# Second cross attention of a two-layer decoder: the key mask is added in PSUM by VectorE in the pass that takes the row maxima, instead of by a bf16 matmul on TensorE

## What is computed

```python
scale = sqrt(128)
q = (text_hidden @ Wq)      # 16 heads of 128
k = (vision_tokens @ Wk)    # 8 key heads of 128, each shared by 2 heads
v = (vision_tokens @ Wv)
scores = einsum('bhtd,bhsd->bhts', q, k) / scale
scores = where(vision_mask[:, None, None, :], scores, -inf)
attn = nan_to_num(softmax(scores, axis=-1), nan=0.0)
out = einsum('bhts,bhsd->bhtd', attn, v)
x = x + out.reshape(B, T, 16 * 128) @ Wo
```

## Time and profile before

| | |
|---|---|
| time, median of 3 runs | 1762.47 us (1761.71 to 1762.89) |
| time of the profiled execution | 1759.19 us |
| its span in the trace | 1757.4 us |
| PE busy, share of the span | 1602.4 us, 91% |
| DVE | 1055.4 us, 60% |
| ACT | 840.0 us, 48% |
| POOL | 740.1 us, 42% |
| mean granted clock of PE | 0.965 of full speed |
| the 64 steps of this sublayer | 1170.4 to some 1522.6 us, about a fifth of the span |

### The profile page before, as it was taken

The page is one execution under the profiler, slowest core; times in us unless marked ns, Lnnn a source line. Parts: engine busy times, 40 slices in busy tenths (PEclk is TensorE's granted clock), DMA queues, the critical chain, the costliest instruction groups (busy, mean ns, idle before and its releaser), DMA issues. The chain is left out here.

```text
span 1757.4 us, 32678 instructions
## 1 busy us (share of the span) xinstructions
PE 1602.4 (91%) x10512; PEld 1276.1 (73%) x10512; DVE 1055.4 (60%) x2390; ACT 840.0 (48%) x2322; POOL 740.1 (42%) x908
## 2 busy tenths in 40 slices
PE   4999979999999998999968888879999999888887
PEld 2565658888888886888845555469999999767675
DVE  3566645656656564555445666545555555589996
ACT  1434437777776775322224444445555555432221
POOL 3666625555455553232321222103333333357775
PEclk9999989999999999899978999989999999999999
DMA  5000020000000000000030000020000000000000
GB/s 219 1 0 0 1 84 3 4 3 1 3 1 3 1 4 1 20 1 1 1 120 1 0 0 0 1 87 7 7 7 7 6 4 1 1 3 12 9 12 13
DMA packets 15399, 28.71 MB, mean 16 GB/s; under 512 B 1489, under 2 KB 11986, under 8 KB 14546
## 3 DMA queue, kind: packets, MB, share of 16 engines
q1 hardware_dynamic: 15314, 27.63, 4.4%
HBM read 25.53 MB, written 2.10 MB: 16 GB/s over the span
## 5 line engine op out<-in xcount | busy, mean ns | idle before, releaser
L1264 POOL TENSOR_TENSOR weights_even<-weights_even,cross_reciprocal 128x512 f32<-128x512 f32 x64 | 67.1, 1049 | 256.4 <-DVE cross_reciprocal L1382 256.4
L1309 ACT ACTIVATE weights_even<-bank,cross_shift 128x128 f32<-128x128 f32 x256 | 90.7, 367 | 102.1 <-DVE cross_shift L1374 102.1
L843 POOL TENSOR_TENSOR weights_odd_early<-weights_odd_early,cross_reciprocal 128x512 f32<-128x512 f32 x64 | 66.7, 1042 | 167.6 <-DVE cross_reciprocal L969 167.6
L1032 PEld LDWEIGHTS bank<-ident,weights_odd_early 128*128 128x128 f32 x768 | 93.7, 141 | 44.4 <-issue 32.7
L1100 PE MATMUL bank<-weights_odd_early 128*128 128x256 f32 x512 | 121.7, 380 | 2.1 <-ACT weights_odd_early L901 2.1
L1032 PE MATMUL bank<-ident,weights_odd_early 128*128 128x128 f32 x768 | 115.1, 273 | 2.2 <-DVE weights_odd_early L957 2.2
L2052 DVE TENSOR_REDUCE grouped_maxima<-bank 128x4 bf16<-128x512 f32 x128 | 82.3, 685 | 56.6 <-PE bank L2118 56.6
L883 ACT ACTIVATE weights_odd_early<-bank,cross_shift,cross_q_rms 128x128 f32<-128x128 f32 x256 | 113.5, 455 | 1.7 <-DVE cross_shift L951 1.7
L1966 ACT ACTIVATE grouped_probs<-bank 128x512 f32<-128x512 f32 x128 | 67.7, 599 | 85.5 <-PE bank L2136 85.4
L1100 PEld LDWEIGHTS bank<-weights_odd_early 128*128 128x128 f32 x512 | 92.2, 190 | 13.9 <-ACT weights_odd_early L901 4.0
L1603 POOL TENSOR_TENSOR mlp_low_inner<-mlp_inner,mlp_high_inner 128x512 fp32r<-128x512 f32 x36 | 48.5, 1347 | 126.3 <-ACT mlp_high_inner L1644 126.3
(11 more groups left out here) (300 smaller groups left out, 5075.5 us busy)
## 6 DMA issues: line engine op xcount, KB each, us to landing
weights_odd_early<-in_weights SPq DMA_DIRECT2D x2, 3072.0 KB, 13.6
weights_even<-in_weights SPq DMA_DIRECT2D x2, 2560.0 KB, 11.8
weights_even<-in_weights SPq DMA_DIRECT2D x2, 1732.0 KB, 8.7
weights_odd_late<-in_weights SPq DMA_DIRECT2D x2, 1536.0 KB, 9.6
x<-in_x SPq DMA_DIRECT2D x4, 512.0 KB, 5.7
out<-mx_result SPq DMA_DIRECT2D x16, 128.0 KB, 1.7
weights_even<-in_weights SPq DMA_DIRECT2D x2, 512.0 KB, 8.6
cross_context<-in_context SPq DMA_DIRECT2D x16, 64.0 KB, 1.7
```

Source lines behind the costliest of these rows:

```text
L843: pool.tensor_tensor(probs[x], probs[x], reciprocal[x][:, :].unsqueeze(2).to_broadcast([P, PER, P]), ALU.mult).then_inc(probs_divided, 1)
L1032: last = pe.transpose(bank[:, j * P:(j + 1) * P], source, core.ident[:, :])
L1264: pool.tensor_tensor(probs[x], probs[x], reciprocal[x][:, :].unsqueeze(2).to_broadcast([P, JOBS, P]), ALU.mult).then_inc(probs_divided, 1)
L1309: last = act.activation(probs[x][:, j, :], bank_scores[x][:, j * P:(j + 1) * P], ACT.Exp, scale=SCALE, bias=shift[x][:, j:j + 1], accum_ou ...
```

## The change

The mask matmul and the diagonals go. The mask is now loaded whole to all 128 partitions (a byte for each batch and key, 2048 columns) and turned into `key_bias`, 128x2048 bf16, by one DVE instruction before the fusing. For each pair, `fetch_mask` copies its 256 columns to `pair_bias`. In `row_maxima` four `tensor_tensor_reduce` instructions, one for each job, take the place of the one reduction: each adds the bias to 128x128 scores, writes the sum back in place to PSUM, and gives the row maximum (never below LEAST_MAX) into one column of `maxima`. A `memset` of one column stands ahead of them. The shift is then computed without the maximum with LEAST_MAX. The score matmuls start their banks themselves. PE's wait for `mask_ready` becomes one of DVE's.

```diff
-        mask = sbuf("mask", [P, BATCHES], mybir.dt.uint8)
-        key_bias = sbuf("key_bias", [P, BATCHES])
-        mask_diagonal = [sbuf(f"mask_diagonal{s}", [P, BOTH, P], BF16) for s in range(2)]
+        mask = sbuf("mask", [P, BATCHES * P], mybir.dt.uint8)
+        key_bias = sbuf("key_bias", [P, BATCHES * P], BF16)
+        pair_bias = [sbuf(f"pair_bias{s}", [P, BOTH * P], BF16) for s in range(2)]
+        pause = sbuf("pause", [P, 1])
...
-            sp.dma_start(mask[:, :], dram["mask"]).then_inc(small_loaded, 16)
+            sp.dma_start(mask[:, :], dram["mask"].partition_broadcast(P)).then_inc(small_loaded, 16)
...
-            def make_mask(p, s):
-                dve.wait_ge(scores_filled, nonneg(GROUPS * (p - 1)))
-                for k in range(BOTH):
-                    last = dve.tensor_scalar(mask_diagonal[s][:, k, :], core.ident[:, :],
-                                             core.column(key_bias, BOTH * p + k), None, ALU.mult)
-                last.then_inc(mask_ready, 1)
+            def fetch_mask(p, s):
+                dve.wait_ge(max_ready, nonneg(GROUPS * (p - 1)))
+                dve.tensor_copy(pair_bias[s][:, :], key_bias[:, bass.ds(p * BOTH * P, BOTH * P)])\
+                   .then_inc(mask_ready, 1)
...
+                dve.wait_ge(mask_ready, p + 1)
                 dve.wait_ge(scores_filled, i + 1)
-                dve.tensor_reduce(maxima[x][:, :], four(bank_scores[x]), AX.X, ALU.max).then_inc(max_ready, 1)
+                dve.memset(pause[:, :], 0.0)
+                for j in range(JOBS):
+                    scores = bank_scores[x][:, j * P:(j + 1) * P]
+                    last = dve.tensor_tensor_reduce(scores, scores, pair_bias[s][:, j % BOTH * P:(j % BOTH + 1) * P],
+                                                    1.0, LEAST_MAX, ALU.add, ALU.max, maxima[x][:, j:j + 1])
+                last.then_inc(max_ready, 1)
                 dve.wait_ge(max_ready, i + 1)
-                dve.tensor_scalar(shift[x][:, :], maxima[x][:, :], LEAST_MAX, -SCALE, ALU.max, ALU.mult)\
-                   .then_inc(shift_ready, 1)
+                dve.tensor_scalar(shift[x][:, :], maxima[x][:, :], -SCALE, None, ALU.mult).then_inc(shift_ready, 1)
...
-                pe.matmul(bank_scores[x][:, :], core.ones_bf[:, :],
-                          mask_diagonal[s][:, :, :].unsqueeze(1).to_broadcast([P, PER, BOTH, P]),
-                          start=True, stop=False)
                 for j in range(JOBS):
                     last = pe.matmul(bank_scores[x][:, j * P:(j + 1) * P], qT[x][:, j, :], contextT[s][:, j % BOTH, :],
-                                     start=False, stop=(j == JOBS - 1))
+                                     start=True, stop=True)
```

More of the change, by code:

```diff
@@ L1341, in _ @@
             dve.wait_ge(small_loaded, 16)
-            dve.tensor_scalar(key_bias[:, :], mask[:, :], 1.0, -NEG, ALU.subtract, ALU.mult)\
-               .then_inc(key_bias_ready, 1)
+            with nc.allow_low_precision("zero, or without bound"):
+                dve.tensor_scalar(key_bias[:, :], mask[:, :], 1.0, -NEG, ALU.subtract, ALU.mult)\
+                   .then_inc(key_bias_ready, 1)
             dve.wait_ge(key_bias_ready, 1)
@@ L1367, in make_low_heads, with row_maxima @@
                                   ALU.subtract).then_inc(heads_low, 1)
-            def row_maxima(i, x):
+            def row_maxima(i, x, p, s):
+                dve.wait_ge(mask_ready, p + 1)
                 dve.wait_ge(scores_filled, i + 1)
-                dve.tensor_reduce(maxima[x][:, :], four(bank_scores[x]), AX.X, ALU.max).then_inc(max_ready, 1)
+                dve.memset(pause[:, :], 0.0)
[4 more added lines that the diff above has]
+                last.then_inc(max_ready, 1)
                 dve.wait_ge(max_ready, i + 1)
-                dve.tensor_scalar(shift[x][:, :], maxima[x][:, :], LEAST_MAX, -SCALE, ALU.max, ALU.mult)\
-                   .then_inc(shift_ready, 1)
+                dve.tensor_scalar(shift[x][:, :], maxima[x][:, :], -SCALE, None, ALU.mult).then_inc(shift_ready, 1)
             def reciprocals(i, x):
@@ L1403, in step @@
                     if there(i):
-                        row_maxima(i, g % 2)
+                        row_maxima(i, g % 2, t, s)
                     if there(i - 2):
@@ L1414, in step @@
                     if g == 6 and pair_there(t + 1):
-                        make_mask(t + 1, 1 - s)
+                        fetch_mask(t + 1, 1 - s)
                     if g in (2, 4) and pair_there(t - 1):
@@ L1518, in step @@
                     if there(i):
-                        if g == 0:
-                            pe.wait_ge(mask_ready, t + 1)
                         scores(i, g % 2, s)
@@ L2622 @@
     arrays["grouped_rows"] = np.concatenate([values["L1_attn_bv"], values["L1_attn_bo"]])[None, :]
-    arrays["mask"] = values["mask_BxS2_bf1"].T.view(np.uint8)
+    arrays["mask"] = values["mask_BxS2_bf1"].view(np.uint8).reshape(-1)
     for n, w in enumerate(packed_weights(values)):
```

## The result

| | before | changed |
|---|---|---|
| median | 1762.09 us (4 runs) | 1785.22 us (4 runs, 1783.61 to 1789.72) |
| ratio | 1 | 1.0153, 95% interval 1.0137 to 1.0168 |
| span of the profiled execution | 1757.4 us | 1781.8 us |
| first to last opening of the 64 steps | 345.24 us | 372.88 us |
| mean granted clock of PE | 0.965 | 0.967 |

The change made the kernel slower by 1.5%, some 23 us by the medians and 27 by the ratio. The prediction was 1800 in a range of 1777 to 1836: sign and range held, the loss was forecast too large. Within the trace the 64 steps account for all of it: 27.64 us more between the first and the last opening, while the rest of the program, of which the change touches only the mask's load and the bias ahead of the fusing, differed by 3 us the other way.

A forecast was written before the change was run, and what follows sets the result against it. PE's queue and DVE's chain to add_output were taken to tie; 8T - 6.66 a pair, 64T - 53.3 for eight, gave +37.6 us at T = 1.42, so 1796.8, or 1800 as a median; range 1777 to 1836.

The forecast's parts named there:

- Two chains arrive together: At add_output in a plain step: DVE's chain to the low heads and PE's own queue tie, slack about nothing.
- 4.62 + T: Length of steps g = 2 and 5, closed by ACT's late copy_qT, against 5.70 before.
- T: On DVE, from first pass's start to last read's end; taken as 1.42 us, where the reduction was 0.69.
- T - 1.08: Change in us of each g = 2 and 5 step, twice in a pair.
- the 0.08 for the memset: On DVE, delay from the memset's start to the first pass: 0.08 us a step.
- 4.45 + T: Length of a plain step, against 5.27 before; 5.87 by the forecast.
- reads nearly free: Rival on DVE's accumulator reads: T from 0.92 to 1.23, +6 to +25 us, 1768 to 1788; chance 0.12.
- 64T - 53.3: Change in us over all 64 steps (eight pairs); +37.6 at T = 1.42.
- The forecast of g = 0 and g = 4: Steps where DVE comes from scale_slice: 4.95 + T against 5.58, and 5.83 + T against 6.42.
- Covers: At the start, the bias instruction of some 2.1 us is covered by DVE catching up: 0 taken, bounds 0 and 3.
- Nothing overlaps on DVE: Rival: DVE's passes and reads run one after another, T = 1.97, +72.8 us, 1835; chance 0.17.
- Clock: Rival: PE's idling drops the granted clock, up to 44 us a pair; 0.04 together with things not seen.

The follow-up runs named there:

- no_mask: The kernel before with the mask matmul left out and nothing in its place; 0.9952 of the kernel before.
- passes_only: The kernel before, mask matmul kept, with DVE's memset and four passes (adding zeros) in place of the one reduction; 1.0212 of the kernel before.
- two_passes: one_wait with one bias addition for all four jobs, then the old reduction, in place of memset and four passes; 1.0266 of the kernel before.
- low_first: one_wait with make_low_heads ahead of row_maxima in DVE's queue; 1.0281 of the kernel before.
- no_shift: one_wait with passes scaled and taking the minimum, so their accumulator is the shift and the shift instruction goes; 1.0046 of the kernel before.
- one_wait: The changed kernel, but DVE waits for mask_ready only in g = 0 of each pair; 1.0126 of the kernel before.

## Why the prediction was right, and where it was off

- **Two chains arrive together, and DVE's becomes the later one.** Right, and shown: removing PE's 0.21 alone gives 5.06 (no_mask), DVE's half alone costs its full length (passes_only), a path longer by 0.33 makes a step longer by 0.32 (two_passes). It was incomplete: there are three chains, and the third, over the exponentials and `copy_probsT`, parts from the second only in low_first and no_shift. It closes the plain steps of those two, and in the changed kernel it ends together with the low heads' chain, so that these alone close the step is not shown. The missing chain is the step that failed for g = 2 and 5. The prediction let ACT's `copy_qT` close them at 4.62 + T; what closes them is `copy_probsT`, behind ACT's `copy_hT`, and they take 5.89, 0.44 more than a plain step, as before the change. The earlier trace rows could have said so: `copy_qT` ends at 1317.00, 0.32 ahead of the opening that it was to close. That term was to be T - 1.08 and is T - 0.82 like the plain one: 16 x 0.26, 4 us too little.
- **T.** This is the term that was mis-sized. 1.42 was taken from between two neighbours; the rows give 1.10, from 1328.13 to 1329.23. The pass of 0.21 was right (0.22 to 0.25 from start to start), but the read adds next to nothing, since it starts with the next pass. Also the 0.08 for the memset is nothing. Together 0.40 too much a step, 64 x 0.40, 26 us. The place of T was right: 4.45 + T with T less the memset, 1.02, is 5.47, measured 5.45. The rival "reads nearly free", T from 0.92 to 1.23, is what happened; its total, 1768 to 1788, holds the measured one, but only together with the next point.
- **The sum.** 64T - 53.3 with 1.02 gives 12 us; measured in the steps were 27.6. The sum missed the g = 2 and 5 term (4), the second wait ahead of the memset in the written-out pairs (23 steps by 0.14, 3 us), the stretched shift (7 steps by 0.5, 3 us), the jump back with the half clock behind it (4.3) and the first step (1). So two errors stood against each other: T 26 us too long, and 16 us of things not seen. That the range held is in part luck: with T right and nothing else the forecast would have been 1774, below its lower end. The forecast of g = 0 and g = 4 was close: 5.97 and 6.85 by the formula, 6.0 and 6.76 measured.
- **Covers.** The bias in one instruction of 2048 columns took 1.23 us, not 2.1, and DVE had caught up with ACT after four subtractions. Counted from PE's first load of the fusing, the first step opened 0.3 us later than before. So that cost was near the 0 taken. The first step itself is 1.34 us longer, some 0.9 of it by the granted clock, which was 0.50 there: its scores took 1.66 until the next weight load, where they took 1.03.
- **"Nothing overlaps on DVE".** Fell: passes of 0.33 start 0.25 apart and a read starts together with the next pass. The Trainium skill, "VectorE: DVE Perf Modes", section "The DRAIN you can't avoid", has the next instruction start only when the pipe is empty, but adds what the prediction left out, that an instruction which is not held starts earlier; the trace shows such early starts. What the same page says in "Two Vector instructions with no wait between them", that an instruction with an accumulator output is two, the trace bears out: 256 passes and 256 reads.
- **Clock.** 0.99 in the stretch, and PE's idle time of 0.4 us in most steps did not bring it down: that rival fell. But the prediction named a granted clock below 1.00 as a sign of being wrong, and this sign came in a small way: the clock was 0.50 in the first step and again behind PE's one stop of nearly 4 us, some 2.5 us of the 27.6 in all.

What stays open: which of DVE's two chains closes the plain step of the changed kernel, why the half-clock stretch reaches into the first step in some executions, whether the instruction DMA is what DVE waits for at the jump back, and why 353 instructions cost so much more there than 227.

## What to carry to other kernels

When two engines' queues tie within a tenth of a microsecond, work taken from one and given to the other costs its full length, whatever the busy shares (98% and 56% of the earlier trace rows) say; follow each chain from one opening of the step to the next, including the one through the third engine. Where a helper stands in the receiving engine's queue can be worth more than the whole change: `scale_slice`, moved to a place where DVE waits anyway, gave 0.5%, as much as taking the mask away altogether. And look at code in a loop and written out apart: a second wait, the jump back and the meeting with another engine cost differently there.

## What the runs showed of the hardware

- On DVE a `tensor_tensor_reduce` of 128x128 out of PSUM and back, with its accumulator read, takes 0.25 us when several follow each other (starts at 1328.35, .59, .84); on ACT an exponential of 128 columns with its read takes 0.35. Neither the second nor plain neighbours gave the first.
- Five memsets of one column take 0.04 us more than one (first pass at 1.35 against 1.31 of the step), although the shift, a small instruction with an input, lets the next start 0.08 later.
- A second semaphore wait ahead of DVE's memset, with the one that is met last on an instruction of its own, cost 0.14 us each time (passes at 1.45 against 1.31 of the step, and gone with one_wait); ahead of the old reduction, in g = 3 of the written-out pairs before, 0.07 (1.59 against 1.52).
- A DVE tensor_scalar of four columns in SBUF took 0.63 to 0.73 instead of 0.17 us in the seven steps in which it began inside POOL's L710, and one of 256 columns 1.27 instead of 0.39 when it began 0.08 ahead of POOL's division, but 0.39 when it began 0.16 ahead. Both ended 0.02 to 0.15 behind POOL's instruction. Not all are held: passes out of PSUM (0.29 to 0.33) and one-column instructions inside POOL's L708 (0.15) kept their time.
- Behind a loop's jump back DVE was 0.27 us late with 227 instructions in the body and stood for 2.80 with 353.
- After TensorE had stood for nearly 4 us and gone on for 1.3 us, its granted clock was 0.50 where it had been 1.00; eight score matmuls took 1.74 instead of 1.0 us there. Idle times of 0.4 us in most steps were followed by no such fall.
